# Routed experts of a six-layer kernel: ScalarE's silu behind the copies, VectorE's routing split, half of an expert's sum one block earlier

## The reference, cut to what matters

```python
def _L1_ffn_ref(x, Wg, Wu, Wd, Wr, temperature):
    inh = sigmoid(x @ Wr / temperature)                 # 8 values a row
    in_zone = (inh >= GOLDEN_LOWER) & (inh <= GOLDEN_UPPER)
    distance = abs(inh - GOLDEN_CENTER)
    weights = exp(-distance / 0.1) * in_zone
    no_expert = sum(weights) < 1e-08
    fb = exp(-distance / 0.3)
    fb_w = fb * (fb is one of the row's two largest)
    fb_w = fb_w / max(sum(fb_w), 1e-08)
    weights = where(no_expert, fb_w, weights)
    weights = weights / max(sum(weights), 1e-08)
    gate = einsum('btd,edf->betf', x, Wg)               # 256 x 256 for each of 8 experts
    up = einsum('btd,edf->betf', x, Wu)
    h = silu(gate) * up
    e_out = einsum('betf,efd->betd', h, Wd)             # 256 x 256 again
    return einsum('bte,betd->btd', weights, e_out)

x = x + _L1_ffn_ref(_layernorm(x), ...)
```

## Time and profile before

| | before |
|---|---|
| median of 3 runs | 3290.34 us |
| profiled execution | 3289.3 us |
| its span | 3287.5 us |
| TensorE busy | 3219.2 us, 98% |
| VectorE busy | 2549.7 us, 78% |
| ScalarE busy | 2191.2 us, 67% |
| GpSimd busy | 2190.4 us, 67% |

### The profile page before, as it was taken

The page is one execution under the profiler, slowest core; times in us unless marked ns, Lnnn a source line. Parts: engine busy times, 40 slices in busy tenths (PEclk is TensorE's granted clock), DMA queues, the critical chain, the costliest instruction groups (busy, mean ns, idle before and its releaser), DMA issues. The chain is left out here.

```text
span 3287.5 us, 110332 instructions
## 1 busy us (share of the span) xinstructions
PE 3219.2 (98%) x36167; PEld 2545.4 (77%) x36176; DVE 2549.7 (78%) x7870; ACT 2191.2 (67%) x6621; POOL 2190.4 (67%) x4233
## 2 busy tenths in 40 slices
PE   9999999999999999999999999999999989999999
PEld 7888888888766776777777777777776678888888
DVE  6677777777788767888888878888877877777777
ACT  5777777777656647777777777777775534445454
POOL 4666666666566447777777777777766775665665
PEclk9999999999999999999999999999999999999999
DMA  3111111111212232111111111111126720000000
GB/s 100 55 55 55 55 55 55 55 55 55 69 51 70 86 114 59 43 47 48 46 48 45 47 45 45 50 45 47 47 64 159 182 90 14 13 13 13 13 13 14
DMA packets 275886, 183.73 MB, mean 56 GB/s; under 512 B 116797, under 2 KB 272661, under 8 KB 275749
## 3 DMA queue, kind: packets, MB, share of 16 engines
q1 hardware_dynamic: 271109, 177.36, 18.8%
q10 hardware_dynamic: 4640, 4.59, 0.5%
HBM read 141.41 MB, written 36.21 MB: 54 GB/s over the span
## 5 line engine op out<-in xcount | busy, mean ns | idle before, releaser
L1264 ACT ACTIVATE probs_a<-s_ps_a,neg_max_a 128x257 f32<-128x257 f32 x1024 | 473.5, 475 | 83.2 <-DVE neg_max_a L1384 78.4
L1318 POOL TENSOR_SCALAR probs_a<-probs_a,gated_a 128x256 f32<-128x256 f32 x1024 | 470.7, 479 | 26.5 <-POOL gated_a L1327 26.4
L1384 DVE TENSOR_REDUCE neg_max_a<-s_ps_a 128x1 f32<-128x257 f32 x1024 | 424.0, 414 | 0.0
L574 POOL TENSOR_SCALAR probs_i<-probs_i,inv_sum_i 128x256 f32<-128x256 f32 x510 | 242.2, 488 | 134.8 <-DVE inv_sum_i L738 130.3
L1383 DVE TENSOR_TENSOR self_s_a<-s_ps_a,mask_a 128x32 f32<-128x32 f32 x1024 | 185.7, 181 | 135.3 <-PE s_ps_a L1107 135.2
L553 ACT ACTIVATE probs_i<-s_ps_i,neg_max_i 128x257 f32<-128x257 f32 x512 | 235.9, 474 | 58.4 <-DVE neg_max_i L812 56.7
L392 PE MATMUL a_ps_i<-w_k_i,ctx_t_i 128*128 128x256 f32 x1024 | 252.8, 390 | 0.0
L1134 PE MATMUL c_ps_a<-w_v_a,ctx_t_a 128*32 128x256 f32 x4096 | 247.6, 382 | 0.0
L379 PE MATMUL c_ps_i<-w_v_i,ctx_t_i 128*128 128x256 f32 x1024 | 247.5, 379 | 0.0
L3069 POOL TENSOR_TENSOR hidden_e<-gate_p,own_p 128x256 f32<-128x256 f32 x192 | 142.7, 748 | 148.4 <-ACT gate_p L3301 125.9
L1100 PE MATMUL b_ps_a<-ctx_t_a,w_qk_a 128*128 128x256 f32 x1016 | 241.3, 380 | 0.0
(11 more groups left out here) (452 smaller groups left out, 9506.6 us busy)
## 6 DMA issues: line engine op xcount, KB each, us to landing
ctx_t_i<-in_ctx_t SPq DMA_DIRECT2D x128, 256.0 KB, 2.7
ctx_t_a<-in_ctx_t SPq DMA_DIRECT2D x128, 256.0 KB, 2.7
mask_a<-in_L_xattn_mask SPq DMA_DIRECT2D x512, 4.0 KB, 1.5
v_bd_a<-v_self_a SPq DMA_DIRECT2D x512, 8.0 KB, 1.8
x_tok_i<-in_x SPq DMA_DIRECT2D x32, 128.0 KB, 2.0
x_res_i<-in_x SPq DMA_DIRECT2D x32, 128.0 KB, 2.5
x_after<-y_tok_i SPq DMA_DIRECT2D x32, 128.0 KB, 1.8
x_tok_d<-x_after SPq DMA_DIRECT2D x32, 128.0 KB, 2.2
```

The lines of the kernel that those rows point to most:

```text
L574: pool.tensor_scalar(probs[:, i, 0:2 * P], probs[:, i, 0:2 * P], inv_sum[:, i:i + 1], 1.0, ALU.mult, ALU.mult).then_inc(probs_ready, 1)
L1264: act.activation(probs[:, t, :], s_ps[:, g, 0:K], ACT.Exp, bias=neg_max[:, t:t + 1], accum_out=row_sum[:, t:t + 1]).then_inc(exp_done, 1)
L1318: pool.tensor_scalar(probs[:, t, 0:2 * P], probs[:, t, 0:2 * P], gated[:, t:t + 1], 1.0, ALU.mult, ALU.mult).then_inc(probs_ready, 1)
L1384: dve.tensor_reduce(neg_max[:, 4 * f + g:4 * f + g + 1], s_ps[:, g, 0:K], AX.X, ALU.max, negate=True).then_inc(max_ready, 1)
```

## The change

ScalarE's silu 11 comes after the copies in every block (it did in block 0). VectorE's two comparisons move behind join 11 of block 1, the totals and weights of the routing behind join 11 of block 2. GpSimd's `route_pairs` comes before `hide` 11. The tile `y` is doubled by the expert's parity, and the waits for it are one expert laxer. The second half (n = 1) of expert e-1 is taken at the end of block e, right behind the down joins that complete it; the first half (n = 0) stays at the start of the next block. In block 2 the end of the block takes both halves of expert 0 and then the second half of expert 1.

```diff
-        self.y = [sb(f"y{n}", [P, 2, D]) for n in range(2)]
+        self.y = [[sb(f"y{n}{m}", [P, 2, D]) for m in range(2)] for n in range(2)]
@@ gpsimd
-                hide(i, e, 11)
                 if e == 1:
                     route_pairs(i)
+                hide(i, e, 11)
                 hide(i, e, 21)
@@ scalar
         def down_last(i, e):
-            act.wait_ge(taken, count(i, e - 1, 2))
+            act.wait_ge(taken, count(i, e - 2, 2))
             act.wait_ge(down_full, down_count(i, e, 3))
-            down_copy(y[0][:, :, P:D], down_chain[e % 2])
+            down_copy(y[0][e % 2][:, :, P:D], down_chain[e % 2])
@@
-                else:
-                    silu(i, e, 11)
                 act.wait_ge(joined, joined_count(i, e - 1, 21))
                 act.wait_ge(chain_full, count(i, e, 4, 2))
                 copy(parts.second, chain[e % 2])
@@
                     down_copy(parts.down_second, down_chain[(e - 1) % 2])
-                if e == 0:
-                    silu(i, e, 11)
+                silu(i, e, 11)
                 silu(i, e, 21)
@@ vector
             link(i, 8, dve.tensor_scalar(none[:, :], total[:, :], TINY, None, ALU.is_lt))
 
+        def route_compared(i):
             dve.tensor_tensor(quad(ahead), by_pair(fb, True), by_pair(fb, False), ALU.is_gt)
             link(i, 9, dve.tensor_tensor(quad(tied), by_pair(fb, True), by_pair(fb, False), ALU.is_equal))
@@
         def down_join(i, e, n, full, source, copy, kept):
-            dve.wait_ge(taken, count(i, e - 1, 2, n // 20))
+            dve.wait_ge(taken, count(i, e - 2, 2, n // 20))
@@ (down_join and take then use y[..][e % 2])
                 if e == 2:
                     route_ties(i)
                     route_fallback(i)
-                    route_totals(i)
-                    route_weights(i)
                 if takes and e not in (0, 2):
-                    take(i, e - 2, 1)
                     take(i, e - 2, 0)
                 dve.wait_ge(second_full, count(i, e))
                 dve.wait_ge(copied, copy_count(i, e, 1))
                 join(i, e, 11, second_ps, parts.first)
-                if takes and e in (0, 2):
-                    take(i, e - 2, 1)
+                if e == 1:
+                    route_compared(i)
+                if e == 2:
+                    route_totals(i)
+                    route_weights(i)
                 dve.wait_ge(seventh_full, count(i, e, 2))
                 dve.wait_ge(copied, copy_count(i, e, 6))
                 join(i, e, 21, seventh_ps, parts.second)
                 dve.wait_ge(chain_full, count(i, e, 4, 1))
                 dve.wait_ge(copied, copy_count(i, e, 7))
                 join(i, e, 22, chain[e % 2], parts.seventh)
-                if takes and e in (0, 2):
+                if takes and e == 0:
                     take(i, e - 2, 0)
                 if follows:
                     down_joins(i, e - 1)
+                if e == 2:
+                    take(i, 0, 1)
+                    take(i, 0, 0)
+                if follows and e != 1:
+                    take(i, e - 1, 1)
                 if begins:
                     sum_down(e)
@@ after the last turn
         hide_last(LAST, E - 1)
-        take(LAST, E - 2, 1)
         take(LAST, E - 2, 0)
         finish()
```

More of the change, by code:

```diff
@@ L3465, in down_join @@
             at = (n % 10 - 1) * P
-            dve.tensor_tensor(y[n // 10 - 1][:, :, at:at + P], source[:, 0:HALF].rearrange("p (t n) -> p t n", t=2), kept[:, :, :], ALU.add).then_inc(down_joined, 1)
+            dve.tensor_tensor(y[n // 10 - 1][e % 2][:, :, at:at + P], source[:, 0:HALF].rearrange("p (t n) -> p t n", t=2), kept[:, :, :], ALU.add).then_inc(down_joined, 1)
         def down_joins(i, e):
@@ L3491, in take @@
                 before_sum = x_tok[2 * n + t][:, :] if e == 0 else acc[n][:, t, :]
-                last = dve.scalar_tensor_tensor(out=acc[n][:, t, :], in0=y[n][:, t, :], scalar=weight[:, 2 * n + t, e % E:e % E + 1], in1=before_sum, op0=ALU.mult, op1=ALU.add)
+                last = dve.scalar_tensor_tensor(out=acc[n][:, t, :], in0=y[n][e % 2][:, t, :], scalar=weight[:, 2 * n + t, e % E:e % E + 1], in1=before_sum, op0=ALU.mult, op1=ALU.add)
             last.then_inc(taken, 1)
```

## The result

The kernel after took 3264.14 us, the median of 4 runs (3262.35 to 3265.56), beside 3291.02 (3287.35 to 3293.09) for 4 runs of the kernel before: a ratio of 0.9919, 95% interval 0.9902 to 0.9936. The span of the profiled run went from 3287.5 to 3261.8 us, 25.7 less.

A forecast was written before the change was run, and what follows sets the result against it. TensorE, busy 98% of the span, was taken as the bound, so only its gaps counted. Turns gave 5 x 2.6 + 2.4 + 2.6 + 1.5 = 19.5 us off 3289.3, plus 1.0 for the median: 3270, range 3259 to 3284.

The forecast's parts named there:

- The waits of `w_sum[1]` and `down_3`: TensorE's losses per turn: 1.67, 1.39 and 0.43 us in blocks 1, 2, 5; 0.29 each in blocks 1 and 3.
- the three waits go in full, gain 3.49, price 0: Blocks 1, 2, 5: silu 11 behind the copies removes every wait of `w_sum[1]`'s product, 3.49 us a turn, at no cost.
- the gross: All the time per loop turn that the change may touch, in blocks 1, 2, 3 and 5: 4.07 us.
- The new losses: Added per turn: 0.3 us in block 0, 0.15 in 1, 0.1 in 3, 0.8 in 5, 0.1 in 6; 1.45 together.
- Block 1: Join 11 at about T+5.0 (T: block start), comparisons to T+6.5, joins to T+7.8, wanted T+8.31; loss 0.15 us (0 to 1.0).
- The port: VectorE and GpSimd lock each other out of SBUF: takes pitched 0.40 or about 0.87 us, block 2's six 2.4 to 5.2.
- rival 1: Port makes every bound high: 2.2 us a turn lost, 3307; chance 0.04 above 3297, 0.10 for 3284 to 3297.
- Turn 0 and turn 1: Gains outside the ordinary turns: turn 0 gives 1.5 us (-1.5 to 5), turn 1 gives 2.4.
- the slow stretch: Turn 0, block 2: matmuls at the lower clock behind a 3.2 us wait; its going saves 1.6 us.
- the third rival: Nearly all gaps close: new losses only 0.5 us a turn, turn 0 gives 5, time 3260; chance 0.14.
- half of it: Half of the 17 us slowdown expected if the port makes every bound high, given as 3297 us.
- Rival 2: Half the gain returns in blocks 1 (0.9 us, comparisons keep 0.95) and 5 (1.3): net 1.35 a turn, 3279; chance 0.24.

The follow-up runs named there:

- take_behind: The kernel after, with the take at the end of block 4 moved behind block 5's `hide_last`: 3258.57 us, ratio 0.9907 to the kernel before.
- take_twice: The kernel after, with every take at a block's end done a second time into a spare tile: 3290.44 us, ratio 1.0002 to the kernel before.
- deviation_later: The kernel after, with GpSimd's `deviation` of block 4 moved behind block 5's sums of hidden values: 3262.88 us, ratio 0.9917 to the kernel before.
- silu_back: The kernel after, with silu 11 ahead of the copies again (block 0 aside): 3267.83 us, ratio 0.9939 to the kernel before.
- silu_alone: The kernel before, with only ScalarE's silu 11 moved behind the copies: 3270.29 us, ratio 0.9942 to the kernel before.
- half_joined: The kernel after without its second-half take at the block's end; block 0 takes that half behind join 11, block 2 as changed: 3259.01 us, ratio 0.9907.
- sums_earlier: take_behind plus, in turn 0, `sum_down` 3 to 7 behind join 11 and `sum_down(2)` behind block 3's `hide_last`: 3253.95 us, ratio 0.9890.
- half_back: The kernel after, with the second half taken with the first at the next block's start (block 0: behind join 22; block 2 as changed): 3271.59 us, ratio 0.9941.

## Why the prediction was right, and where its sizes were off

The mechanism held: direction, place and the new bound. The sizes held less well: 3264.14 lies 0.9 below the stretch of 3265 to 3275 that had a chance of 0.48, in the one below 3265 that had 0.14. Point by point:

*The waits of `w_sum[1]` and `down_3`.* Blocks 1, 2, 3 and 5 had 1.96, 1.39, 0.29 and 0.43 to give by the sum, and gave 1.97, 1.40, 0.28 and 0.44 (block 5 by its 9.17 in take_behind). But the sentence "the three waits go in full, gain 3.49, price 0" is true of the change and not of the silu: alone it gave 1.8 to 2.4, since joins 22 and the down joins were late behind the wait. I had put the whole gain on one edit because its cause was the named releaser.

*What the gross left out.* Block 0 gave 0.12 and block 6 0.15. 9.39 and 9.32 stood in the trace; I counted only blocks with a wait that I had listed. Gross 4.36 for 4.07. The kernels that take the second half inside block 0, behind join 11 or 22, have 9.38 to 9.41 there in turns 2 to 6, and those that take it at the end of block 7 have 9.27 or 9.28 (take_twice aside): so the 0.12 is that half leaving block 0. VectorE's routing steps from `inh` to `dist` take 1.80 for 1.96 there; why, no run shows.

*The new losses, the mis-sized term.* I had 1.45 a turn: 0.3 in block 0, 0.15 in 1, 0.1 in 3, 0.8 in 5, 0.1 in 6. Measured: 0.71, all in block 5. There the shift of `hide_last` was 1.01 for my 0.96 and the loss 0.71 for 0.8. In blocks 1 and 6 my own working gave a time before the point where it is due (T+7.8 against 8.31, T+5.4 against 5.66), and I still added a tenth or more; for block 0 I had worked out no such time at all. Block 3 was the close one: forecast T+2.7 and T+5.4 to 5.7 against 5.66, measured 2.70 and 5.37. The margin is small (take_twice finds it), but inside it the cost is zero. That is 0.74 a turn, and with the 0.29 of the gross it makes the 1.03 by which 3.65 is above my 2.62; five times 1.03 is 5.2 of the 6.4 us by which the sum of 19.5 was low (turn 0 holds 0.8 more).

*Block 1.* Join 11 ended at T+5.86, not at 5.0: `total` to `none` held a 0.63 and the takes lasted 1.69 beside GpSimd's sums. The comparisons made up for part of it: 0.41 each in place of 0.90 and 0.95, now that they run where GpSimd is idle (I had counted 1.5 for both). They ended at T+6.52, and I had T+6.5. Join 22 ended at T+8.09, 0.3 later than my T+7.8, with 8.31 due. That two errors of mine partly cancelled here is luck.

*The port.* The bound that mattered, 0.40 or 0.87 a take, went the low way: 0.42 in the six, 0.40 in the last pair of them (3057.44 to 3058.23). The high bound was misread, too: four takes in 3.08 are 0.77 each, and 0.87 is the length of a whole pair. With 0.77 the worst case for the six is 4.6 and not 5.2, so rival 1 was somewhat overpriced. Where GpSimd works, it is as the rival said: a pair takes 1.35 (deviation_later) or 1.69 (block 1). The Trainium skill (SBUF — State Buffer, section "SBUF: two separate sides") has the two engines lock each other out for a whole instruction; the sums' rows agree, with 0.73 stretched to 0.91 and the takes with them. The pair beside `deviation` doesn't: it starts 0.28 behind the start of that 1.02 us instruction, and lasts 0.87. The same is seen in each of turns 1 to 6, and in those of silu_back and take_twice.

*Turn 0 and turn 1.* The 1.6 for the slow stretch is more than the earlier trace rows gives (2.30 - 1.25 = 1.05). The rest lies in the product ahead of it, which starts at 2668.69 and is followed by the next at 2670.30, 1.61 for a pitch of 0.87:

```profile
2668.69 1.81 PE L3142 MATMUL bank_e<-x_sum_p,w_sum_p 128*128 128x256 f32 x4 [3.25 <-ACT second_p L3284]
```

Turn 0 gave 2.28 for 1.5, with the shape mostly as forecast: a wait of 1.35 before `w_sum[4]` of block 2 for "about 2", so that the block gave 3.55 for 3.0, with no slow stretch; 1.20 lost in block 3 for 1.5; block 1 gave 0.67 for 0.5. Not forecast were 0.57 from block 0 and 0.44 lost in block 4, and blocks 5 and 6 lost 0.87 together for 0.5. Turn 1 gave 2.51 for 2.4; its block 0 went from 9.72 to 10.55, 0.83 for the 0.8 of a take pair that I had charged.

*The rivals.* The time lies between my case (loss 1.45) and the third rival (0.5); the losses of rival 1 didn't come, since GpSimd does stand still, waiting for `hide_last`, while the takes run. Its "half of it" should read 3299 and not 3297. Rival 2 named block 1, where the comparisons were to keep 0.95; they did not. That the copy waited for the silu is shown by silu_alone.

What I had not asked is whether each part pays. The half at the block's end, to which I gave no sum of its own, costs 5 us by the blocks: 0.71 a turn in block 5 against 0.4 to 0.7 in blocks 0 and 1, and 4 us in turns 0 and 1, where it meets `sum_down`. It is not the idea that costs but those places: with the take of block 4 moved, it brings 0.4 to 0.7 a loop turn (take_behind), and with `sum_down` moved as well the kernel is 5 us faster than half_joined by the medians (sums_earlier).

## What to carry to other kernels

Take the gaps of a steady stretch from the distance of like points in neighbouring blocks, not from the list of waits: the list had 0.27 a turn less, and shows none of what stands behind a wait. When a wait goes, look at what the second slowest engine delivers in the same block: here a third to a half of a gain hung on the reordering that came with it. Where a moved step ends before its due point by your own working, put down zero and keep the doubt for the range. Give each part of a change its own sum, and each place of a part too, since one may cost what the others bring.

## What the runs showed of the hardware

The same kind of stall was followed by a low clock in some turns and not in others. These are TensorE's windows (us, busy, granted clock) of half_back, before, in and behind a wait of 2.06 in block 1 of one turn; the same block with a wait of 1.50 in the other turns has no such stretch.

```profile
2880.00:2886.00 6.00, 6.00 (x40) 1.00 0.00 0
2888.00:2890.00 2.00, 0.04 (x1) 1.00 0.00 0
2890.00:2894.50 4.50, 4.50 (x17) 0.63 0.10 33
```

In sums_earlier the stretch behind a wait of 2.12 in turn 0 shows 0.54:

```profile
2670.80:2673.80 3.00, 3.00 (x8) 0.54 0.00 0
```

That is the lower level, 1.2 of 2.4 GHz, for nearly all of 3.00 us, and goes with 12.31 in that block, where half_joined, with a wait of 1.50, has 11.02. But in the kernel after a stall of 2.70 in turn 0's block 5 was followed by full clock:

```profile
2697.00:2703.00 6.00, 6.00 (x40) 1.00 0.01 3
```

So a stall of 2 us may cost some 1.4 to 1.7 us more behind it (an estimate: 3.00 x 0.46 in sums_earlier; in half_back 13.14 - 10.91, less the 0.56 of longer wait, is 1.7); which stalls do, these runs don't settle.

An instruction of 128x4 elements on GpSimd that lasts 1.02 us did not slow a VectorE take pair that ran beside it, while sums of 128x256 do (1.35 for the pair). And two comparisons of 128x256 went from 0.90 and 0.95 to 0.41 each when they were moved from beside GpSimd's sums to where GpSimd is idle.
